# Attention and gated feed-forward on one core: six blocks' queries behind the context, and the looks, one weight sum and the second block's attention placed anew

## The chip, the cores and the metric

One core of a Trainium2 chip. The metric is the device time of one launch in microseconds; a lower one is better. TensorE (PE) multiplies matrices into PSUM, VectorE (DVE), ScalarE (ACT) and GpSimd (POOL) work elementwise, SyncE (SP) issues the transfers.

## The reference

Linear attention (no softmax) over 4096 tokens of width 256, a residual sum and a layer norm, then a gated feed-forward net and a second residual sum and norm. "tlin" is a product with a weight matrix, then a scale for each output channel.

```python
# x: (1, 4096, 256); wq, wk, wv: (64, 256); wo: (256, 64)
Q = x @ wq.T;  K = x @ wk.T;  V = x @ wv.T
energy = einsum('bnd,bne->bde', K, V)
context = einsum('bnd,bde->bne', Q, energy) * sqrt(3 / 64)
x = layernorm(x + context @ wo.T)
h = silu(tlin(x, w1, s1)) * tlin(x, w2, s2)            # hidden width 1024
h = gelu(tlin(h, h1, sh1)); h = gelu(tlin(h, h2, sh2)) # exact gelu
x = layernorm(x + tlin(h, w3, s3))
```

All weights of the feed-forward net are small integers, and wq is plus or minus 1/16.

## The kernel before, in words

The tokens are eight blocks of 512. Every engine runs a list of instructions written out by hand, and semaphores alone tie the lists together: an engine stands at an instruction until its semaphores have come, and all behind it stands too. SP's list of transfers is one such list.

**Two-part products.** An operand is split into a rounded high part (ScalarE: hi, high_x, hi_of_q, hi_of_transposed) and a low rest (VectorE: lo, low_x, lo_of_q, lo_of_transposed). TensorE multiplies both with weights that are exact in the short format. Whether they are, the kernel looks itself: ScalarE sums the low bits of each piece of weights (`bits`, L562: bits_of_w12, bits_of_whole for loaded units, bits_of_sums for sums of weights). For each of seven stages TensorE adds the sums up (flag_sum, L1203), VectorE makes a flag of them (flag_out, L864), and TensorE loads it (load_flag, L1215) and jumps by it (stages_from, L1225).

**Front** (L1417). For each block f: keys and values (kv_products, L1150), copied by VectorE, and their energy, one 64 x 64 sum over all blocks (energy, L1166). Queries are four matmuls a block, two on xhi and two on xlo (q_pieces, L1134; piece n belongs to block n // 4). Up to `Q_BETWEEN` a block's queries stand between two rounds of keys and values. Behind the last energy come T1 (energy times wo, L1430) and the attention of block 0, tile by tile (attention_tile, L1178; a tile is 128 tokens, and there are four in a block). VectorE adds x and takes the statistics of each tile (normalised_tilewise, L1057), GpSimd makes the inverse deviation and the shift (L483, L477), ScalarE normalises tiles 0 and 1 (normalise_tile, L627), VectorE tiles 2 and 3, and TensorE transposes each tile (transposed_first, L1449). Block 1's attention is done in two halves (attention_half, L1453) among them. The queries of the other blocks are copied out by ScalarE (raw_q, L602), those of blocks 4 to 7 on their way to DRAM.

**Gate layer** (l1, L1251): sixteen tiles of four matmuls for a block, half of them for silu (ScalarE, L633), half for the gate (VectorE, L932). Tile t >= 4 needs a bank that silu or gate has left (l1_free, L1238). Within block 0's layer, behind tile 9, stand the transposes of block 1 (L1197, TR1_AFTER); they need it normalised (stats and normalise on VectorE, L905 and L924, with inverse_deviation on GpSimd between them, L454).

**Hidden layers.** Two 1024 x 1024 products for two blocks at a time, each by seven products of half size with sums of weights and of activations (product, L1298; differences, L499). The sums of weights are made once: GpSimd combines a loaded unit in four operations (combine, L439), SP stores it to DRAM (store_unit, L319), and each product loads its sum into one of three ring slots (load_ring, L324). Two of seven products take a quarter of the weights unchanged, which SP copies from DRAM to DRAM (relay_hidden, L307).

In the `combine` and in ScalarE's list the order that matters below is this:

```python
combine(0)                                   # GpSimd
inverse_deviation_tilewise(0)
combine(1)
inverse_deviation(0, 1)
pool.wait_ge(norm_done[0], 1)
combine(2)
```

## Time and profile before

| | |
|---|---|
| median of 3 runs | 653.43 us (651.85 to 653.5) |
| the profiled execution, its own time | 653.65 us |
| its span | 651.9 us |
| TensorE busy | 637.2 us, 98% of the span |
| VectorE, ScalarE, GpSimd busy | 485.7, 410.7 and 282.1 us |
| granted TensorE clock | 0.998 of full speed |
| moved by DMA | 103.89 MB, 159 GB/s over the span |

In a timeline a line is a run of like instructions: start, length, engine, line of the code, what is written from what, how many, and in brackets how long the engine had been idle and who released it. "idle" is shown from about 0.15 us on. Lengths of neighbouring instructions on ScalarE and VectorE overlap by about 0.1 us, so distances between starts are the better measure.

### The profile page before, as it was taken

Reading aid. Unit: us, or ns where it says so; the run is one execution under the profiler, and the core shown is the slowest. Engines: PE = TensorE matmul, PEld = TensorE weight load, DVE = VectorE, ACT = ScalarE, POOL = GpSimd, SP = SyncE. Lnnn points to the kernel's source line nnn. Section 1 sums busy time; section 2 is a strip of 40 time slices with the busy share of each in tenths; the row PEclk is TensorE's granted clock in tenths of the full one; section 3 lists DMA queues with packets and bytes.
Section 4 is the critical chain, followed back from the end, with each engine's and each line's share of the span. In section 5 each row is a group of like instructions: output and inputs, shape, how many; then the busy total and the mean of one; then the engine's idle time right before and its main releaser. Section 6 shows DMA issues by size and latency. Waiting matters only on the chain.

```text
span 651.9 us, 9251 instructions
## 1 busy us (share of the span) xinstructions
PE 637.2 (98%) x3191; PEld 534.6 (82%) x3191; DVE 485.7 (75%) x717; ACT 410.7 (63%) x696; POOL 282.1 (43%) x226
## 2 busy tenths in 40 slices
PE   8989999999999999999999999999999999999995
PEld 6867788878889888888889888888889888888885
DVE  4677598789664997798655898698754899488476
ACT  5488789658761666557662657656763457666554
POOL 0367999295000663097000565079000367068034
PEclk9999999999999999999999999999999999999999
DMA  8989999764320036633330035734330015444201
GB/s 327 394 325 341 372 380 348 285 255 164 130 67 1 1 118 220 211 130 130 130 129 1 1 97 167 250 126 168 130 129 2 1 28 188 173 135 160 94 1 66
DMA packets 24370, 103.89 MB, mean 159 GB/s; under 512 B 2224, under 2 KB 3312, under 8 KB 16496
## 3 DMA queue, kind: packets, MB, share of 16 engines
q1 hardware_dynamic: 24032, 102.98, 44.5%
q8 instruction: 29, 0.48, 0.3%
q10 hardware_dynamic: 288, 0.26, 0.1%
q14 instruction: 21, 0.17, 0.1%
HBM read 87.51 MB, written 23.07 MB: 170 GB/s over the span
## 4 chain that ended last, share of the span: by engine, by line
PE 72%; DVE 3%; POOL 1%; issue 1%; ACT 1%; POOLq 0%; DVEq 0%; ACTq 0%
PE ps L1322 49%; PE ps L1262 13%; PE ps L1376 8%; DVE R L944 1%; DVE xr L928 1%; PE ps L1194 1%; PE ps L1182 1%; PE ps L1399 0%; ACT R L674 0%; DVE U L963 0%; POOL rstd L488 0%; POOL quarter L516 0%; ACT quarter L720 0%; POOL rstd L459 0%; POOL quarter L525 0%
## 5 line engine op out<-in xcount | busy, mean ns | idle before, releaser
L1322 PE MATMUL ps<-R,ring 128*128 128x512 f32 x1792 | 410.1, 390 | 1.6 <-DVE fsum L866 1.2
L1322 PEld LDWEIGHTS ps<-R,ring 128*128 128x128 f32 x1792 | 335.2, 188 | 71.6 <-DVE fsum L866 1.6
L944 DVE TENSOR_TENSOR R<-quarter,R 128x512 fp32r<-128x512 f32 x284 | 261.8, 944 | 62.6 <-ACT R L674 62.2
L674 ACT CAST R<-quarter 128x512 fp32r<-128x512 f32 x288 | 175.4, 616 | 30.6 <-POOL quarter L516 12.6
L1262 PE MATMUL ps<-x1T,w 128*128 128x512 f32 x512 | 119.4, 391 | 1.9 <-ACT sg L640 1.1
L720 ACT ACTIVATE quarter<-U,sc 128x512 f32<-128x512 f32 x96 | 69.5, 724 | 74.2 <-DVE U L963 29.4
L1262 PEld LDWEIGHTS ps<-x1T,w 128*128 128x128 f32 x512 | 95.2, 188 | 23.8 <-ACT sg L640 2.7
L506 POOL TENSOR_TENSOR quarter<-quarter,quarter 128x512 f32<-128x512 f32 x32 | 49.6, 1550 | 97.8 <-ACT quarter L720 91.1
L457 POOL TENSOR_TENSOR ve<-mv,eps 128x4 f32<-128x4 f32 x14 | 5.7, 404 | 181.5 <-DVE mv L921 181.5
L640 ACT ACTIVATE sg<-ps,sc 128x512 f32<-128x512 f32 x64 | 44.0, 689 | 61.3 <-PE ps L1262 61.1
L690 ACT COPY U<-ps 128x512 f32<-128x512 f32 x96 | 56.3, 586 | 31.3 <-PE ps L1322 31.3
L938 DVE SCALAR_TENSOR_TENSOR quarter<-ps,sc,sg 128x512 f32<-128x512 f32 x64 | 47.8, 746 | 23.7 <-ACT sg L640 13.4
L516 POOL TENSOR_TENSOR quarter<-quarter,quarter 128x512 f32<-128x512 f32 x32 | 48.9, 1527 | 16.7 <-DVE quarter L938 12.9
L1376 PEld LDWEIGHTS ps<-w,R 128*128 128x128 f32 x448 | 54.7, 192 | 0.7 <-DVE R L944 0.2
L1376 PE MATMUL ps<-w,R 128*128 128x256 f32 x448 | 55.1, 283 | 0.0
L528 POOL TENSOR_TENSOR quarter<-quarter,quarter 128x512 f32<-128x512 f32 x32 | 50.0, 1594 | 0.0
L525 POOL TENSOR_TENSOR quarter<-quarter,quarter 128x512 f32<-128x512 f32 x32 | 48.8, 1554 | 0.0
L928 DVE TENSOR_SCALAR xr<-xr,mv,rstd 128x256 f32<-128x256 f32 x52 | 35.5, 743 | 4.2 <-POOL rstd L459 4.2
L957 DVE TENSOR_TENSOR U<-ps,U 128x512 f32<-128x512 f32 x32 | 22.0, 690 | 14.7 <-PE ps L1322 14.7
L720 ACT ACTIVATE quarter<-ps,sc 128x512 f32<-128x512 f32 x32 | 22.1, 691 | 12.6 <-PE ps L1322 12.6
L963 DVE TENSOR_TENSOR U<-ps,U 128x512 f32<-128x512 f32 x32 | 21.8, 685 | 8.2 <-PE ps L1322 8.2
L446 POOL TENSOR_TENSOR beside<-unit 128x512 f32<-128x512 f32 x8 | 12.2, 1530 | 29.8 <-ACT junk L569 27.7
(84 smaller groups left out, 383.4 us busy)
## 6 DMA issues: line engine op xcount, KB each, us to landing
ring<-combos SPq DMA_DIRECT2D x56, 1024.0 KB, 4.9
combos<-unit SPq DMA_DIRECT2D x8, 1024.0 KB, 7.1
unit<-in_h1T SPq DMA_DIRECT2D x4, 1024.0 KB, 13.9
xr<-in_x_rows SPq DMA_DIRECT2D x8, 512.0 KB, 6.2
unit<-in_h2T SPq DMA_DIRECT2D x4, 1024.0 KB, 12.7
xT<-in_xT SPq DMA_DIRECT2D x7, 512.0 KB, 8.6
out<-xr SPq DMA_DIRECT2D x7, 512.0 KB, 2.9
w<-w_dram SPq DMA_DIRECT2D x3, 1024.0 KB, 7.5
```

What stands on the lines that cost most here:

```text
L506: nc.gpsimd.tensor_tensor(x12[:, c, :], x12[:, c, :], x11[:, c, :], ALU.subtract).then_inc(t_done, 1)
L516: nc.gpsimd.tensor_tensor(t2[:, c, :], x22[:, c, :], x12[:, c, :], ALU.subtract).then_inc(t_done, 1)
L525: nc.gpsimd.tensor_tensor(x11[:, c, :], t2[:, c, :], x11[:, c, :], ALU.subtract).then_inc(t_done, 1)
L528: nc.gpsimd.tensor_tensor(x21[:, c, :], x21[:, c, :], t2[:, c, :], ALU.subtract).then_inc(t_done, 1)
L674: nc.scalar.copy(R[slot_of(p, u)][:, 0, c, :], quarter[operand_home(p, u)][:, c, :]).then_inc(hi_done, 1)
L690: nc.scalar.copy(U[:, 1 if i == 2 else 0, j, :], ps[:, B + j, :]).then_inc(cp_done, 1)
L720: nc.scalar.activation(quarter[dst][:, j, :], src, ACT.Gelu, scale=sc[:, 2 + l, chunk:chunk + 1]).then_inc(gelu_done, 1)
L938: nc.vector.scalar_tensor_tensor(quarter[dst][:, j % KH, :], ps[:, base + (2 * j + 1) % 4, :], sc[:, 1, j:j + 1], sg[:, j % 2, :], ALU.mul ...
L944: nc.vector.tensor_tensor(r[:, 1, c, :], quarter[operand_home(p, u)][:, c, :], r[:, 0, c, :].bitcast(f32), ALU.subtract).then_inc(lo_done, 1)
L1262: last = nc.tensor.matmul(ps[:, base + t % 4, :], w, view(x1T[beta % 2][:, part, c, :]), start=n == 0, stop=n == 2 * EC - 1)
L1322: last = nc.tensor.matmul(ps[:, bank + j, :], w, view(R[slot_of(p, u)][:, part, k, :]), start=n in (0, 1, 5) and k == 0 and part == 0, sto ...
L1376: last = nc.tensor.matmul(rows_of(b)[:, q, :], view(slot[:, part, k, q * P:(q + 1) * P]), w, start=first and k == 0 and part == 0 and q % ...
```

## The change

**TensorE.** Only block 0's queries and block 1's stand between the rounds of keys and values; those of blocks 2 to 7 follow the last energy. Fifteen of the 24 come before the first transposed tile, three between it and tile 1's, four behind. The jump by the look at w12 stands behind them, ahead of tiles 2 and 3 and of block 1's attention, whose halves change places. Block 6's queries go to bank 2. In product 5 of each first hidden layer the attention of the next two blocks stands behind its third and fourth part in place of behind all four.

**ScalarE.** The casts of x no longer wait for queries (eight buffers in place of four, the last four in the ring's space). raw_q(2) and raw_q(3) stand around a look at w12, behind T1; the normalised tiles 0 and 1 stand behind all looks at w12; the look at unit 1 behind raw_q(7); the looks at sums are split in two; hi_of_q(2) and hi_of_q(3) go to the first hidden layer.

**GpSimd.** The last of unit 0's four operations waits until block 0 is normalised.

**VectorE.** The flag of w12 comes ahead of the normalising of tiles 2 and 3; lo_of_q(2) and (3) go to the first hidden layer.

**SP.** Block 0's rows of x go ahead of unit 0. The two DRAM copies of a hidden layer are apart, each with a flag of its own, and the second comes behind the first ring load, or behind block 2's rows. The ring's first load waits for all queries. Units 5 and 6 go behind ring load 2, unit 7 behind ring load 3.

```diff
-Q_BETWEEN = 4
+Q_BETWEEN = 2
-Q_BANK = (4, 5, 6, 7, 5, 4, 5, 3)
+Q_BANK = (4, 5, 6, 7, 5, 4, 2, 3)
...
+        xhi_at = [x1T_at + 4096 * i for i in range(4)] + [ring_at + 4096 * i for i in range(4)]
+        xhi = [over(f"xhi{f}", xhi_at[f], [P, EC, BLK], f32r) for f in range(NB)]
...
+                if g == 0:
+                    sp.wait_ge(q_ready, NB)
+                if L < 2 and n < 2:
+                    sp.wait_ge(hidden_relayed[L][n], 16)
...
+            load_rows(0)
             load_unit(0)
             load_w12(0)
             load_w12(1)
-            load_rows(0)
...
-            relay_hidden(0)
+            relay_hidden(0, 0)
             load_unit(4)
             store_unit(2)
             load_ring(0)
+            relay_hidden(0, 1)
+            store_unit(3)
             load_ring(1)
+            load_ring(2)
             load_unit(5)
-            store_unit(3)
             load_unit(6)
-            load_ring(2)
+            load_ring(3)
             load_unit(7)
             store_unit(4)
-            load_ring(3)
-            relay_hidden(1)
             load_ring(4)
+            relay_hidden(1, 0)
             load_rows_late(2)
+            relay_hidden(1, 1)
...
             combine(0)
             inverse_deviation_tilewise(0)
+            pool.wait_ge(last_norm[0], TPB - ACT_TILES[0])
+            last_sum(0)
             combine(1)
...
                 silu(0, j, A)
-                if j == 1:
-                    hi_of_q(2)
-                if j == 3:
-                    hi_of_q(3)
                 if j == 0:
                     bits_of_whole(2)
-                if j == 2:
-                    bits_of_sums(0)
+                if 2 <= j <= 3:
+                    bits_of_sums(0, range(j - 2, j - 1))
...
-                if j == 6:
+                if j == 5:
                     bits_of_whole(3)
...
                 silu(1, j, A)
-                if j == 0:
-                    bits_of_sums(1)
+                if j <= 1:
+                    bits_of_sums(1, range(j, j + 1))
...
-                if j == 1:
+                if j == 2:
                     bits_of_whole(4)
-                if j == 4:
-                    bits_of_sums(2)
+                if 3 <= j <= 4:
+                    bits_of_sums(2, range(j - 3, j - 2))
...
-                q_pieces(range(23, 28), view)
+                q_pieces(range(15, 25), view)
                 pe.wait_ge(q_raw, 2)
                 transposed_first(0)
-                q_pieces(range(28, 30), view)
-                transposed_first(1)
-                q_pieces(range(30, 32), view)
+                q_pieces(range(25, 28), view)
                 pe.wait_ge(tile_sum[0], 1)
                 flag_sum(1)
-                transposed_first(2)
-                attention_half(0)
-                transposed_first(3).then_inc(tr_ready, 1)
-                attention_half(1).then_inc(op_ready, 1)
+                transposed_first(1)
+                q_pieces(range(28, 32), view)
...
+                transposed_first(2)
+                attention_half(1)
+                transposed_first(3).then_inc(tr_ready, 1)
+                attention_half(0).then_inc(op_ready, 1)
                 l1(0, A, view, side)
```

TensorE from the sum of the look at w12 on, before (L1194 are transposed tiles, L1182 block 1's attention, L1217 and L1230 the flag's load and the jump):

```order
L1211 MATMUL ps<-lowf,ones 1x4 [waits bits_done,tile_sum0]
L1194 MATMUL ps<-ident,xr 128x128 [waits last_norm0]
L1194 MATMUL ps<-ident,xr 128x128
L1182 MATMUL ps<-T1s,qs_66 128x256 [waits q_raw,qlo_done]
L1182 MATMUL ps<-T1s,qs_66 128x256 x3
L1194 MATMUL ps<-ident,xr 128x128 [waits last_norm0]
L1194 MATMUL ps<-ident,xr 128x128
L1182 MATMUL ps<-T1s,qs_66 128x256 [waits q_raw,qlo_done]
L1182 MATMUL ps<-T1s,qs_66 128x256 x3
L1217 TENSOR_LOAD flag [waits flag_done]
L1217 ISA x2
L1230 COMPARE_AND_BRANCH
```

And in the change (the same lines are L1216, L1199, L1187, L1222 and L1235 there, the queries L1150):

```order
L1216 MATMUL ps<-lowf,ones 1x4 [waits bits_done,tile_sum0]
L1199 MATMUL ps<-ident,xr 128x128 [waits tile_norm0]
L1199 MATMUL ps<-ident,xr 128x128
L1150 MATMUL ps<-xhi_116,wqr 128x512 [waits tile_sum0,xhi_done]
L1150 MATMUL ps<-xhi_116,wqr 128x512
L1150 MATMUL ps<-xlo_124,wqr 128x512 [waits xlo_done]
L1150 MATMUL ps<-xlo_124,wqr 128x512
L1222 TENSOR_LOAD flag [waits flag_done]
L1222 ISA x2
L1235 COMPARE_AND_BRANCH
L1199 MATMUL ps<-ident,xr 128x128 [waits last_norm0]
L1199 MATMUL ps<-ident,xr 128x128
```

The jump has moved from behind the transposed tiles and the attention to ahead of tile 2; tile 1 and four query matmuls now stand ahead of it.

ScalarE from T1 to the first silu, before (L569 are looks, L605 copies of queries, L631 normalised tiles, L625 the cast of the transposed block):

```order
L801 ACTIVATE T1s<-ps 128x256 [waits t1_ready]
L605 COPY q_stage_95<-ps 128x512 [waits q_ready]
L569 ACTIVATE junk,lowf<-w_49 128x1024 [waits bits_done,w12_in1] x2
L605 COPY q_stage_96<-ps 128x512 [waits q_ready]
L631 ACTIVATE xr<-xr,shift,rstd_84 128x256 [waits shift_done] x2
L569 ACTIVATE junk,lowf<-unit_122 128x1024 [waits bits_done,unit_in1]
L605 COPY q_stage_97<-ps 128x512 [waits q_ready]
L625 CAST x1T_63<-ps 128x512 [waits tr_ready]
L625 CAST x1T_63<-ps 128x512
L605 COPY q_stage_98<-ps 128x512 [waits q_ready]
```

And in the change, from the copy behind T1 on (looks L580, copies L614, normalised tiles L640, cast L634):

```order
L614 COPY xr<-ps 128x512 [waits q_ready]
L580 ACTIVATE junk,lowf<-w_49 128x1024 [waits bits_done,w12_in0]
L614 COPY xr<-ps 128x512 [waits q_ready]
L580 ACTIVATE junk,lowf<-w_49 128x1024 [waits bits_done,w12_in1] x2
L640 ACTIVATE xr<-xr,shift,rstd_84 128x256 [waits shift_done]
L614 COPY q_stage_95<-ps 128x512 [waits q_ready]
L640 ACTIVATE xr<-xr,shift,rstd_84 128x256 [waits shift_done]
L614 COPY q_stage_96<-ps 128x512 [waits q_ready]
L634 CAST x1T_63<-ps 128x512 [waits tr_ready]
L634 CAST x1T_63<-ps 128x512
L614 COPY q_stage_97<-ps 128x512 [waits q_ready]
L614 COPY q_stage_98<-ps 128x512 [waits q_ready]
```

The first normalised tile now stands behind two copies and three looks, counted from T1, and the look at unit 1, which stood ahead of the cast, comes behind these rows.

## Rows read from the trace of the kernel before

**Rows 1.** Busy time of a stretch: us, engines' busy us, granted clock, DMA.

```profile
150.00:600.00 450.00, 449.70 (x2200) 380.03 (x2200) 342.61 (x501) 272.60 (x464) 167.09 (x120) 1.00 0.33 113
```

**Rows 2.** TensorE's waits by line: us in total, times, longest.

```profile
PE ps L1322 <- DVE fsum L866: 1.2, 1, 1.2
...
PE ps L1322 <- issue: 0.4, 1, 0.4
```

**Rows 3.** TensorE's timeline: start, us, instruction, xcount, [idle before].

```profile
18.54 1.95 PE L1162 MATMUL ps<-wkv,xT 128*128 128x128 f32 x16
...
22.05 1.95 PE L1162 MATMUL ps<-wkv,xT 128*128 128x128 f32 x16
...
24.54 2.05 PE L1162 MATMUL ps<-wkv,xT 128*128 128x128 f32 x16
...
27.12 2.05 PE L1162 MATMUL ps<-wkv,xT 128*128 128x128 f32 x16
...
34.07 0.40 PE L1145 MATMUL ps<-xlo,wqr 128*128 128x512 f32 x1
...
36.77 0.41 PE L1194 MATMUL ps<-ident,xr 128*128 128x128 f32 x2 [1.37 <-ACT xr L631]
...
39.55 0.38 PE L1194 MATMUL ps<-ident,xr 128*128 128x128 f32 x2
...
41.08 9.53 PE L1262 MATMUL ps<-x1T,w 128*128 128x512 f32 x40 [0.68 <-ACT x1T L625]
50.45 1.03 PE L1194 MATMUL ps<-ident,xr 128*128 128x128 f32 x8
51.24 13.23 PE L1262 MATMUL ps<-x1T,w 128*128 128x512 f32 x56
65.55 4.85 PE L1262 MATMUL ps<-x1T,w 128*128 128x512 f32 x20 [1.08 <-ACT sg L640]
```

**Rows 4.** ScalarE's timeline.

```profile
33.10 1.06 ACT L569 ACTIVATE junk<-w 128x1024 uint8<-128x1024 uint16 x1
...
35.40 0.57 ACT L605 COPY q_stage<-ps 128x512 f32<-128x512 f32 x1
...
39.96 1.07 ACT L625 CAST x1T<-ps 128x512 fp32r<-128x512 f32 x2 [0.67 <-PE ps L1194]
...
58.47 1.90 ACT L569 ACTIVATE junk<-unit 128x2048 uint8<-128x2048 uint16 x1
...
61.12 0.60 ACT L674 CAST R<-quarter 128x512 fp32r<-128x512 f32 x1
...
62.21 0.61 ACT L674 CAST R<-quarter 128x512 fp32r<-128x512 f32 x1
63.77 1.06 ACT L569 ACTIVATE junk<-unit 128x1024 uint8<-128x1024 uint16 x1 [0.95 <-DMA unit<-in_h2T]
```

**Rows 5.** The flag's load near 39.5 us: ns min/median/max, first and last start.

```profile
L1217 PEldq TENSOR_LOAD <-flag x1: 906/906/906, 39.5 to 39.5; - x1
```

**Rows 6.** GpSimd's timeline: tile 0's shift, combine(1), an inverse deviation, an operation of combine(4).

```profile
35.73 0.27 POOL L480 TENSOR_SCALAR shift<-mv,rstd 128x1 f32<-128x1 f32 x1
...
38.96 1.41 POOL L446 TENSOR_TENSOR beside<-unit 128x512 f32<-128x512 f32 x1 [0.19 <-ACT junk L569]
...
43.17 1.29 POOL L452 TENSOR_TENSOR unit<-unit 128x512 f32<-128x512 f32 x1
...
46.34 1.02 POOL L459 TENSOR_TENSOR rstd<-ve,nhalf 128x4 f32<-128x4 f32 x1
...
69.85 1.61 POOL L452 TENSOR_TENSOR unit<-unit 128x512 f32<-128x512 f32 x1
```

**Rows 7.** VectorE's timeline: normalise of block 1.

```profile
48.03 1.37 DVE L928 TENSOR_SCALAR xr<-xr,mv,rstd 128x256 f32<-128x256 f32 x4
```

**Rows 8.** SP's timeline: issue of unit 4's load.

```profile
50.58 0.75 SPq L317 DMA_DIRECT2D unit<-in_h2T  x1
```

**Rows 9.** Transfers issued near 50.6 us: KB each, us to landing.

```profile
unit<-in_h2T SPq DMA_DIRECT2D x1, 1024.0 KB, 13.2
```

More of the change, by code:

```diff
@@ L148, in build @@
         xT = [over(f"xT{f}", r_at + 4096 * f, [P, TPB * E]) for f in range(NB)]
-        xhi = [over(f"xhi{i}", x1T_at + 4096 * i, [P, EC, BLK], f32r) for i in range(4)]
+        xhi_at = [x1T_at + 4096 * i for i in range(4)] + [ring_at + 4096 * i for i in range(4)]
+        xhi = [over(f"xhi{f}", xhi_at[f], [P, EC, BLK], f32r) for f in range(NB)]
         xlo = [over(f"xlo{f}", r_at + 4096 * f, [P, TPB * E], f32r) for f in range(NB)]
@@ L180, in build @@
         unit_out = [sem(f"unit_out{i}") for i in range(NU)]
-        hidden_relayed = [sem(f"hidden_relayed{l}") for l in range(2)]
+        hidden_relayed = [[sem(f"hidden_relayed{l}_{h}") for h in range(2)] for l in range(2)]
         ring_in = [sem(f"ring_in{k}") for k in range(SLOTS)]
@@ L439, in combine @@
             def combine(i):
-                w11, w21, w12_, w22 = (unit[i][:, a, :] for a in range(4))
+                w11, w21, _, w22 = (unit[i][:, a, :] for a in range(4))
                 pool.wait_ge(unit_in[i], 16)
@@ L450, in combine, with last_sum @@
                 nc.gpsimd.tensor_tensor(w11, w21, w11, ALU.subtract).then_inc(combo_step, 1)
+                if i != 0:
+                    last_sum(i)
+            def last_sum(i):
                 pool.wait_ge(combo_step, 3 * i + 3)
-                nc.gpsimd.tensor_tensor(w12_, w12_, w11, ALU.subtract).then_inc(combos_made, 1)
+                nc.gpsimd.tensor_tensor(unit[i][:, 2, :], unit[i][:, 2, :], unit[i][:, 0, :], ALU.subtract).then_inc(combos_made, 1)
             def inverse_deviation(ln, n):
@@ L786, in _ @@
             nc.scalar.copy(wqr[:, :, :], wq[:, :, :]).then_inc(wq_rounded, 1)
-            for f in range(4):
+            for f in range(5):
                 high_x(f)
             hi_of_q(0)
-            high_x(4)
+            high_x(5)
             hi_of_q(1)
-            high_x(5)
-            raw_q(2)
             high_x(6)
-            raw_q(3)
             high_x(7)
@@ L798, in _ @@
             bits_of_w12(0)
-            bits_of_w12(1)
             act.wait_ge(t1_ready, 1)
             nc.scalar.activation(T1s[:, 0, :], ps[:, 3, 0:E], ACT.Copy, scale=CTX_SCALE).then_inc(t1_hi, 1)
-            raw_q(4)
+            raw_q(2)
+            bits_of_w12(1)
+            raw_q(3)
             bits_of_w12(2)
             bits_of_w12(3)
+            normalise_tile(0, 0, 0, 1, tile_norm[0])
+            raw_q(4)
+            normalise_tile(0, 0, 1, 2, tile_norm[0])
             raw_q(5)
-            for q in range(ACT_TILES[0]):
-                normalise_tile(0, 0, q, q + 1, tile_norm[0])
+            hi_of_transposed(0, 6)
+            raw_q(6)
+            raw_q(7)
             bits_of_whole(1)
-            raw_q(6)
-            hi_of_transposed(0, 6)
-            raw_q(7)
             act.wait_ge(cst_in, 16 * NCST)
@@ L980, in hidden @@
                         add_first(L, j)
+                    if L == 0 and j < 2:
+                        lo_of_q(a + j)
                     if j > 0:
@@ L1005, in hidden @@
                         add_fourth(L, j)
-                    if L == 0 and j == 1:
+                    if L == 0 and j == 2:
                         residual1(a, B)
@@ L1325, in product @@
                     last.then_inc(prod, 1)
+                    if side is not None:
+                        side(j)
             def hidden(p, l, view):
@@ L1345, in with_sums, with attention @@
                 product(p, l, 4, view)
-                product(p, l, 5, view)
-                if l == 0 and more:
-                    for i in range(2):
-                        pe.wait_ge(gelu_done, n_gelu(L, 1, 2 * i + 1))
-                        attention_out(a + i, lambda q, at=B + 2 * i: ps[:, at + q // 2, q % 2 * E:(q % 2 + 1) * E])
+                def attention(j):
+                    if j >= 2:
+                        pe.wait_ge(gelu_done, n_gelu(L, 1, 2 * j - 3))
+                        attention_out(a + j - 2, lambda q, at=B + 2 * (j - 2): ps[:, at + q // 2, q % 2 * E:(q % 2 + 1) * E])
+                product(p, l, 5, view, attention if l == 0 and more else None)
                 if p == 0 and l == 1:
```

43 lines of the change are left out of this document (19 added, 24 removed).

## The prediction

> **What bounds the kernel now.** I read the busy time by stretch first. From 150 to 600 us TensorE is busy for 449.70 of 450 us, at a granted clock of 1.00 [rows 1]: in the body nothing but its own matmuls counts, and the change removes none of them. What can be won or lost is idle time of TensorE outside that stretch. The list of its waits names one at the flag sum of the second layer, 1.2 us, and 0.4 us of issue at a stage's start [rows 2]; its timeline shows the others, all early [rows 3]: 1.37 us before the first transposed tile (36.77), 0.68 before the first gate layer (41.08), 1.08 in that layer's second block (65.55). These five are 4.7 us, 0.7% of the span: the most that could be won, were every one to go. A change under 0.3%, some 2 us, can't be told from none here.
>
> **1. The context comes earlier.** A round of keys, values and energy takes 3.51 us with one block's queries in it (18.54 to 22.05), 2.49 just behind such a round (22.05 to 24.54) and 2.58 in a pure run (24.54 to 27.12) [rows 3]. Blocks 2 and 3 leave two rounds, so 3.51 + 3.51 + 2.49 become 2.49 + 2.58 + 2.58: **1.87 us earlier** for everything that hangs on the context: T1, attention of block 0, its sums and statistics. Waits for x don't eat this: by then the last x transfer is long there, and the eight xhi tiles no longer wait for queries. The rows of x go ahead of unit 0 on SP's queue, so unit 0 and both halves of w12 land 512 KB (about 1.3 us) later. They still come before ScalarE must turn to T1, though with only some 0.3 us to spare.
>
> **2. Most of that lead is lost on ScalarE.** It must normalise tile 0 before TensorE can transpose it. Before, both looks at w12's second half (33.10 to 35.40, 2.30 us) lay in time in which the tile's shift wasn't there yet [rows 4]. Now the shift, ready at 36.00 before [rows 6], is there at 34.1, but the order puts ahead of it raw_q(2), a look, raw_q(3) and these two looks. raw_q(3) needs the last query matmul of block 3, which stands where the one of 34.07 stood [rows 3]: 34.07 - 1.87 = 32.2, and the copy can start at about 32.6 and is through at 33.1. Then 2.30 of looks: 35.4; the tile 0.6: 36.0; TensorE starts tile 0 at **36.15** in place of 36.77. From 32.2 TensorE has ten query matmuls of 0.24 (13.23 / 56 [rows 3]), to 34.6, and then idles 1.5 us: the old wait stays.
>
> **3. From there to tile 3.** Before, it was 39.55 - 36.77 = 2.78. Now three query matmuls more lie in it (0.7), 0.2 of waiting for tile 1 goes, and the jump into the next stage stands ahead of tile 2, so that it lies in the chain: load of the flag, compare, branch. No row shows that jump with nothing beside it. Ends: 0.4 us (the issue wait [rows 2]) and 0.9 (the flag's TENSOR_LOAD took 906 ns [rows 5]); I take 0.7, by the 0.68 before 41.08, in which the same look's jump lies. A wait for the flag is not added: flag_sum(1) stands seven instructions ahead, and VectorE now waits for it before it normalises tiles 2 and 3, which are wanted only behind the jump. So tile 3 starts at 36.15 + 2.78 + 0.7 - 0.2 + 0.7 = 40.15, **0.6 later** than before, and the gate layer, which hangs on tile 3 through the casts and the low halves on VectorE, moves by the same 0.6. The trace decides this price against a rule: in the Trainium skill, Advanced Engine Details and Errata, Control Flow Timing, a compare-and-branch is about 108 ns. The compare alone agrees, but what counts here is the load with it. By that rule the jump would be 0.1, and the sum 0.6 lower.
>
> **4. The second block's transposes.** They stand behind ten tiles of the gate layer, reached at 50.45 before, with no wait [rows 3]; now at 51.05. They need block 1 normalised, and its inverse deviation is behind combine(1) on GpSimd, which needs the look at unit 1; combine(1) began at 38.96 [rows 6]. Now ScalarE does it last: tile 3's transpose 40.15; casts 0.41 later (39.55 to 39.96) and 1.07 long; raw_q(6) and raw_q(7), 0.57 each; the look 1.15 (half of 2.30) [rows 4]: 43.9, GpSimd 44.0. combine(1) took 5.50 (38.96 to 44.46); at 1.61 an operation it would be 6.5 [rows 6], and I take 5.5, since what VectorE does beside it is again gates and statistics with PSUM inputs. The inverse deviation is 1.3 (0.28 + 1.02), normalise 1.37 [rows 6, 7]: 44.0 + 5.5 + 1.3 + 1.4 + 0.1 = 52.3. TensorE **waits 1.25 us** where it did not wait. The point for gate(3), queued behind normalise on VectorE, is 54: not reached. The Trainium skill, SBUF — State Buffer, Who interferes with whom, has a VectorE instruction with two SBUF inputs block a GpSimd read altogether; none stands in this stretch, so by it combine(1) would be 4 x 1.37 = 5.5 as well, and the 6.5 is what a lo beside it would cost.
>
> **5. The wait at 65.55 goes: -1.08.** silu(1, 2) was late because ScalarE stood 0.95 us for unit 4 (63.77) [rows 4]. unit 4 now has one relay of 1 MB ahead of it instead of two, and the look stands one silu later; two query casts have left ScalarE and VectorE there.
>
> **6. A new wait in the same place.** ScalarE starts the second block's first silu a tile (0.945: 13.23 over 14 [rows 3]) and 0.2 after TensorE starts the block. Tile 12 needs silu(1, 4), and ahead of its end now lie four silu-and-hi pairs of 1.09, both parts of sums(1) 2.65, the look at unit 4 1.05, the long part of sums(2) 2.0 and the silu 0.67 [rows 4]: 10.7. That is 12.0 with the handover, against 12 x 0.945 = 11.3: **+0.65**.
>
> **7. At nothing.** The queries' casts in the second layer's start (ScalarE and VectorE, 1.2 and 1.4 us) lie beside product matmuls with some 3 us in hand, and so does unit 5, which lands some 10 us later. The attention of two blocks moves into product 5 with the same matmuls; VectorE's residuals wait less. If this cover were gone, product 3 would wait by what is missing. The wait at the flag sum, 1.2 us, hangs on TensorE's own product 6, VectorE's add, gelu and eight GpSimd differences, all behind that product, so it moves with it and stays.
>
> Sum: +0.6 + 1.25 - 1.08 + 0.65 = **+1.4 us**. Profiled execution 653.65 + 1.4 = 655.05; it stands 0.22 above the median, 653.43: **654.8**.
>
> **Rivals.** (a) The lead is kept. Were tile 0 ready when TensorE is (34.7 in place of 36.15), tile 3 and the gate layer would come 0.85 earlier than before, and with combine(1) in time and tile 12 free, -0.85 - 1.08 = -1.9 is left: 651.5; with a jump of 0.1 it is 650.9. For it: T1 1.87 earlier is sure. Against it: ScalarE's order is fixed, and the 2.30 of looks can't be passed. Chance 0.12, most of which would have to come through some step that I priced too high. (b) Slower by more than 2 us, through the transfers. store_unit(0) leaves behind last_sum(0), which waits for block 0's last norm and takes another 1.3 us: some 40. store_unit(1) leaves behind combine(1), at 49.5 in place of 44.5 [rows 6]. unit 4 landed 50.58 + 13.2 = 63.8, 19.3 behind store_unit(1) [rows 8, 9]. With a relay less I expect 15.4 behind it, 64.9, wanted at 65.8. Were the relay to save nothing, it would land at 68.8 and hold ScalarE, and so tile 12, for 3 us: 657.8. It decides from 0.9 us of delay on; ring(1), behind the second relay and with 1.5 us in hand, adds to it. Chance 0.28, with combine(1) at 6.5 or a second long wait counted in. (c) The Control Flow rule holds, as a mechanism: the flag is loaded while the queries still run, and the jump is hidden. Then tile 3 comes at 39.55, the four terms are 0, 1.25, -1.08 and 0.65, and the time is 654.2. Chance 0.15, inside no change. (d) That the change doesn't do what it says: only if the rounds were held by x; but from 18.54 to 27.12 they follow each other with no idle time shown [rows 3], so under 0.02.
>
> **Numbers.** Forecast, within 0.3%: 0.60, with 653 to 656 as its own range. Faster 0.12, slower 0.28. Range: down to 651.5, where half of (a) is left out; up to 657.5, which takes most of (b).
>
> **What the profile after would show.** Key and value rounds of 2.5 us and T1 at 29.4; ScalarE's first normalised tile at 35.4 directly behind a look; TensorE idle about 1.4 us before the first transposed tile and 0.4 to 0.9 before the third, with the flag's load there; the gate layer's first matmul at 41.5 to 41.7; a wait of 1 to 1.5 us at the second transposes, named after VectorE's normalise; none by unit 4; one of about 0.7 before tile 12 of the second block, released by silu. A first transposed tile at 35 would make step 2 wrong, no wait at the second transposes step 4, a ScalarE look released by a DMA near 66 would be rival (b).

## The result, and the profile after

The changed kernel takes 655.4 us (median of 7 runs, 655.02 to 656.32), the one before 653.43 in the runs beside it (651.85 to 654.22). The ratio is 1.0039, with a 95% interval of 1.0028 to 1.0050, or 1.8 to 3.3 us slower; it is estimated from all the runs and isn't the ratio of the two medians, which is 1.0030. The forecast was 654.8, inside no change. So the total is 0.6 off, and by the forecast's own line of 0.3% the kernel is slower, though the interval begins just under that line. Profiled spans are 653.6 and 651.9; I account for these 1.7 us, since the rows come from them.

The stretch in which nothing was to happen, 150 to 600 us (columns as in [rows 1], 449.70 busy before):

```profile
150.00:600.00 450.00, 448.83 (x2195) 379.06 (x2194) 340.87 (x500) 270.99 (x463) 165.77 (x119) 1.00 0.33 113
```

TensorE's timeline after, the rows that answer to [rows 3], and then the waits behind 140 us:

```profile
14.54 1.95 PE L1167 MATMUL ps<-wkv,xT 128*128 128x128 f32 x16
...
17.03 2.05 PE L1167 MATMUL ps<-wkv,xT 128*128 128x128 f32 x16
...
19.62 2.05 PE L1167 MATMUL ps<-wkv,xT 128*128 128x128 f32 x16
...
28.90 0.70 PE L1439 MATMUL ps<-wo,ET 64*128 64x256 f32 x2
...
32.10 0.40 PE L1150 MATMUL ps<-xlo,wqr 128*128 128x512 f32 x1
...
36.04 0.41 PE L1199 MATMUL ps<-ident,xr 128*128 128x128 f32 x2 [1.37 <-ACT xr L640]
...
39.22 0.38 PE L1199 MATMUL ps<-ident,xr 128*128 128x128 f32 x2
...
40.37 9.91 PE L1267 MATMUL ps<-x1T,w 128*128 128x512 f32 x40 [0.30 <-ACT x1T L634]
51.12 1.06 PE L1199 MATMUL ps<-ident,xr 128*128 128x128 f32 x8 [0.84 <-DVE xr L934]
...
51.94 16.60 PE L1267 MATMUL ps<-x1T,w 128*128 128x512 f32 x72
69.16 1.20 PE L1267 MATMUL ps<-x1T,w 128*128 128x512 f32 x4 [0.62 <-ACT sg L649]
...
73.28 5.60 PE L1327 MATMUL ps<-R,ring 128*128 128x512 f32 x24
```
```profile
142.08 16.66 PE L1327 MATMUL ps<-R,ring 128*128 128x512 f32 x72 [1.54 <-DVE fsum L872]
...
183.17 7.04 PE L1267 MATMUL ps<-x1T,w 128*128 128x512 f32 x30 [0.18 <-issue]
...
310.90 1.06 PE L1199 MATMUL ps<-ident,xr 128*128 128x128 f32 x8 [0.44 <-DVE xr L934]
```

Rounds follow each other in 2.49 and 2.59 us, the gate layer starts at 40.37 with 0.30 of idle time, the second transposes wait 0.84, tile 12 of the second block 0.62, and nothing waits for unit 4. Three waits are new or longer behind 140 us: 1.54 at the flag sum (1.16 in before's timeline), 0.44 at 310.90, and another 0.43 a pair later, at 461.51. One of 0.18 stands ahead of the second pair's gate layer, put down to issue: time in which the engine waited for nothing that the profile shows.

To set the two runs side by side I count from the third round of keys and values, which began at 11.51 before and 11.02 after, since x came at different times (in the kernels with the change's front it began anywhere from 11.00 to 12.09). The balance, each stretch as after minus before (product 0 is the first product of the first hidden layer, the "first pair" runs from there to the gate layer of the second pair):

| stretch | before | after | difference | forecast |
|---|---|---|---|---|
| start to 3rd round | 11.51 | 11.02 | -0.49 | |
| to the first transposed tile | 25.26 | 25.02 | -0.24 | -0.62 |
| to the gate layer | 4.31 | 4.33 | +0.02 | +1.2 |
| to the second transposes | 9.37 | 10.75 | +1.38 | +1.25 |
| to product 0 | 23.41 | 22.16 | -1.25 | -0.43 |
| first pair | 108.98 | 109.89 | +0.91 | 0 |
| from there to w3's row near 642 | 458.23 | 459.55 | +1.32 | 0 |

They sum to +1.65. The front (rows two to five) was forecast at +1.4 and comes out at -0.09; the loss lies behind it, in what I had put at nothing. These are single executions. In e1, e3, e10, e11 and e14 below, which have the front of the kernel after, product 0 starts 61.90 to 62.26 behind the third round, and 62.26 to 62.35 in the kernel before, e2 and e9, which have the old one. So the front wins between nothing and 0.45 us.

### The profile page after: what moved, and what is told of

It reads as the page before. It is cut to its first block and busy times, and to the rows that moved or that the text cites. A ratio compares the mean times of both kernels' runs of the same rounds, so it can differ in the third digit from the quotient of the medians.

```text
span 653.6 us, 9254 instructions
## 1 busy us (share of the span) xinstructions
PE 638.0 (98%) x3191; PEld 534.5 (82%) x3191; DVE 485.4 (74%) x717; ACT 408.8 (63%) x696; POOL 280.5 (43%) x226
## 5 line engine op out<-in xcount | busy, mean ns | idle before, releaser
L580 ACT ACTIVATE junk<-unit 128x1024 uint8<-128x1024 uint16 (+1 forms) x16 | 23.9, 1494 | 9.4 <-DMA unit<-in_h1T 9.4
```

## The experiments

"The weave" is the change's new order in product 5, with the attention of the next two blocks between and behind its last two parts. All ratios are against the kernel before, which took 652.48 to 653.43 in its sets of runs. Theory A is that VectorE's and ScalarE's work, put elsewhere in the hidden layers, is late and holds TensorE there; its rivals are given with each.

### The weave alone and the change without it

VectorE's timeline near product 5 of the second pair, after:

```profile
272.44 0.69 DVE L963 TENSOR_TENSOR U<-ps,U 128x512 f32<-128x512 f32 x1 [1.50 <-PE ps L1327]
...
275.04 2.35 DVE L897 TENSOR_TENSOR xr<-ps,xr 128x1024 f32<-128x1024 f32 x2
...
309.38 1.37 DVE L934 TENSOR_SCALAR xr<-xr,mv,rstd 128x256 f32<-128x256 f32 x4
```

and before:

```profile
271.16 0.69 DVE L957 TENSOR_TENSOR U<-ps,U 128x512 f32<-128x512 f32 x1 [0.53 <-PE ps L1322]
...
273.76 2.35 DVE L891 TENSOR_TENSOR xr<-ps,xr 128x1024 f32<-128x1024 f32 x2
...
308.10 1.37 DVE L928 TENSOR_SCALAR xr<-xr,mv,rstd 128x256 f32<-128x256 f32 x4
```

The pair's product 0 started at 227.64 after and at 227.34 before, so each of these three links (part 3's sum, block a's and b's residual sums, block b's normalise) is 0.98 us later against it. Half of the attention now runs on TensorE ahead of part 3 of product 5 (the fourth and last, counted from 0), and everything behind part 3's sum follows. e1 puts the attention back in the kernel after; e2 makes this one edit in the kernel before, together with the one on VectorE that belongs to it in the change: block a's residual sum one step later in the first pair.

```diff
 e1, against after:
-                product(p, l, 5, view, attention if l == 0 and more else None)
+                product(p, l, 5, view)
+                if l == 0 and more:
+                    attention(2)
+                    attention(3)
```

> The changed kernel with the attention of two blocks back behind all of product 5. Theory A (the weave makes VectorE's chain late): in pairs 1 and 2 the attention of the first block delays the product's last part by 0.95 us, and with it VectorE's last low half, both residual sums, all that follows, and the second transposes of the next layer; the waits of 0.44 and 0.43 us there go, each pair is 0.65 us shorter, 1.3 us in all: about 654.1. Rival B (the loss behind 300 us is TensorE's own, from switching between two kinds of matmul twice as often): the switching goes too, so this run alone gives the same 654.1, but without the waits it removes TensorE's busy time would have to fall. Rival C (transfers or the front are the cause): no change from 655.4.

> The kernel before with nothing but the weave of the attention into product 5 (and VectorE's first residual sum one step later in the first pair). Theory A: +1.3 us in pairs 1 and 2, nothing or up to 0.5 in the first pair: 654.7 to 655.2, with a wait of about 0.4 at the second transposes of each later pair. Rival C: no change from 653.4.

e1: 654.53, ratio 1.0021 (1.0012 to 1.0029). e2: 654.19, 1.0017 (1.0006 to 1.0027). TensorE's timeline at the second pair's second transposes, without the weave (e1):

```profile
310.20 1.91 PE L1199 MATMUL ps<-ident,xr 128*128 128x128 f32 x16
```

and with the weave alone (e2):

```profile
310.33 1.06 PE L1194 MATMUL ps<-ident,xr 128*128 128x128 f32 x8 [0.46 <-DVE xr L928]
```

Counted from product 0 to the first matmul behind the second transposes, the two later pairs take 84.1 us each with the weave and 83.4 without, from either side (e1 83.42 and 83.43; e2 84.10 and 84.07; before 83.42 twice, after 84.08 and 84.07). So the weave costs 0.65 a pair, 1.3 in all, and it is shown by undoing it and by doing it alone. In the first pair the weave changes nothing in the kernel before: its last product starts 101.35 behind product 0 in e2 and 101.30 before.

In time e1 won less than the 1.3: its first pair took 110.65 for the 109.89 of the kernel after. Of this, 0.69 is a wait for the rows of x of block 3, which were issued at 113.43 and at 113.01 in the kernel after. Whether the missing weave has a part in that isn't shown; e4 below has the weave and waits 0.61 there. Both medians were off their forecasts by about half a microsecond (654.1, and 654.7 to 655.2), so it is the pairs in the traces that show the 0.65, with the medians in line.

### The weave with VectorE's sums ahead

If the late link is VectorE's order and not TensorE's, taking block a's and b's residual sums ahead of the last low half should win the time back with the weave in place.

```diff
                 for j in range(KH + 1):
                     if j < KH:
                         add_fourth(L, j)
...
+                    if l == 0 and p > 0 and more and j == KH:
+                        residual1(a, B)
+                        residual1(b, B + 2)
                     if j > 0:
                         lo(p, u0 + 7, j - 1)
-                if l == 0 and p > 0 and more:
-                    residual1(a, B)
-                    residual1(b, B + 2)
```

> The changed kernel, weave kept, but in pairs 1 and 2 VectorE adds the two residuals ahead of the last low half instead of behind it, in time in which it waits for ScalarE anyway. Theory A: VectorE is about 1.3 us earlier from there, the waits at the second transposes go, 1.3 us less: 654.1. Rival B (TensorE's own switching): the weave is still there, so no change from 655.4.

654.54, 1.0021 (1.0012 to 1.0029). The pairs are 83.45 and 83.44, with no wait: so the late link is the order on VectorE. But the first pair took 111.04, with a new wait. Its timeline, and the transfers issued between 100.5 and 100.9 us (KB each, us to landing):

```profile
111.87 5.72 PE L1327 MATMUL ps<-R,ring 128*128 128x512 f32 x24 [1.74 <-issue]
```

```profile
ring<-combos SPq DMA_DIRECT2D x1, 1024.0 KB, 11.1
```

Ring load 5 was issued at 100.64, landed at 111.7, and product 5 wanted it at 110.1. In the kernel after it went at 100.56 and took 9.0: there by half a microsecond. Before, it went at 97.76 and took 8.6: there more than four early. The change has used up this transfer's reserve, and then an execution in which it takes 1 to 2 us more pays for it (below, e5 paid 0.61). e3 doesn't touch this stretch.

### The queries between the rounds again

```diff
-Q_BETWEEN = 2
+Q_BETWEEN = 4
...
-                q_pieces(range(8, 10), view)
+                q_pieces(range(16, 18), view)
...
-                q_pieces(range(10, 15), view)
+                q_pieces(range(18, 23), view)
...
-                q_pieces(range(15, 25), view)
+                q_pieces(range(23, 25), view)
```

> The changed kernel with the queries of blocks 2 and 3 back between the rounds of keys and values, all else as changed. If the context's place is what made the front 0.58 us shorter in spite of two new waits, everything from T1 to the gate layer's end comes later by what ScalarE's fixed list makes of it: T1 1.9 later, the first transposed tile 1.5 later (37.6), the gate layer's end 1.5 later: 656.9. Rival: the looks on ScalarE hide the context's lead, and the front stays as it is to within 0.3: 655.4.

658.37, 1.0075 (1.0059 to 1.0092), 1.5 above the forecast. The first transposed tile came at 37.73 and product 0 at 76.49 instead of 73.28. Of these 3.21 us, 0.92 is x, which came late in this execution (third round at 11.94). Another 0.77 is the first transposed tile, counted from the third round (25.79 for 25.02). The rest, 1.45, lies between this tile and the gate layer (5.78 for 4.33), and there TensorE ran at a lower clock:

```profile
36.62 0.47 PE L1150 MATMUL ps<-xhi,wqr 128*128 128x512 f32 x1 [1.70 <-DVE xr L1083]
37.73 0.41 PE L1199 MATMUL ps<-ident,xr 128*128 128x128 f32 x2 [0.64 <-ACT xr L640]
...
39.08 1.11 PE L1150 MATMUL ps<-xhi,wqr 128*128 128x512 f32 x2
```

Two query matmuls took 1.11 us here and 0.71 in the kernel after (37.40). The granted clock was 0.60, 0.50, 0.50 and 0.70 in the four microseconds from 39 on, behind idle times of 1.70 and 0.64 us that lay close together; 0.50 is the lower level, 1.2 GHz. The kernel after has 1.37 of idle time there and the full clock. Four microseconds at a mean of 0.57 are up to 1.7 us of lost clock, so the 1.45 is accounted for. The place of the two blocks' queries was worth 0.7 to 1.1 us to the first transposed tile (it stands 24.66 to 25.06 behind the third round in the ten traces with the queries where the change has them). The forecast had 1.5 for that and nothing for the clock. Of the other five executions the one with the lowest mean clock, 0.992, took 659.90, and the two with the highest, 0.997, took 658.14 and 656.46. Pair and flag waits were those of the kernel after (0.44, 0.47, 1.55).

### The jump in its old place

```diff
                 q_pieces(range(28, 32), view)
+                transposed_first(2)
+                attention_half(1)
+                transposed_first(3).then_inc(tr_ready, 1)
+                attention_half(0).then_inc(op_ready, 1)
...
-                transposed_first(2)
-                attention_half(1)
-                transposed_first(3).then_inc(tr_ready, 1)
-                attention_half(0).then_inc(op_ready, 1)
                 l1(0, A, view, side)
```

> The kernel after, with the second block's tiles 2 and 3 and its two attention halves back ahead of the jump, so that nothing but the gate layer stands behind the jump, as before. Theory (a jump costs where the flag is read late): before, the flag's load took 906 ns and 0.68 us stood open at the gate layer; here the flag comes early, as in the kernel after (load of 0.31 us), so the wait at the gate layer stays under 0.3 us, its first matmul starts at 40.2 to 40.5 and the time is that of the kernel after, 1.002 to 1.004 of before. Rival (a jump costs what it costs wherever weight loads follow it, and the rounds behind it merely paid it in the kernel after): 0.6 to 0.8 us open at the gate layer, its first matmul at 40.9 to 41.2, and the ratio 0.001 above the kernel after's.

The gate layer started at 39.93 with 0.29 of idle time; counted from the third round that is 28.93, and 29.35 in the kernel after. The flag's load, after, in e5, and before in [rows 5] (906 ns):

```profile
L1222 PEldq TENSOR_LOAD <-flag x1: 311/311/311, 37.7 to 37.7; - x1
```

```profile
L1222 PEldq TENSOR_LOAD <-flag x1: 312/312/312, 38.1 to 38.1; - x1
```

From ScalarE's first cast of the transposed block to the gate layer's first matmul it is 0.73 us in both, and 1.12 before (39.96 to 41.08). So the jump costs nothing there in either place, it did cost some 0.4 before, and the theory is right that its place isn't what made it dear. What makes a load last 0.3 or 0.9 us is not settled: it follows the flag by 0.2 us before (flag at 39.3) as in the kernel after (37.5), and by 0.9 in e5 (37.2). All kernels with the change have the short load, e4 with its queries moved back too: 308 to 323 ns here and 302 to 418 at the next stage. The kernels before, e2 and e9 have the long one, 898 to 913 and 862 to 1169. The time was 655.67, 1.0055 (1.0041 to 1.0069), not under the kernel after's: here too the time went behind the stretch tried, 0.61 at ring load 5 (110.48) and 0.81 at tile 12.

### The look at unit 1 earlier

ScalarE stood idle 2.30 us ahead of its cast near 39.6 in the kernel after, and had the look at unit 1 behind it. e6 is e1 with this:

```diff
             raw_q(5)
+            bits_of_whole(1)
             hi_of_transposed(0, 6)
             raw_q(6)
             raw_q(7)
-            bits_of_whole(1)
```

> The kernel without the weave (654.5) and with ScalarE's look at h2's unit 1 ahead of its cast of tile 6's high part, into the 2.30 us that ScalarE stood idle there. Theory: the look starts some 2 us earlier (39.6 instead of 41.55), combine(1) on GpSimd starts at 41.0 instead of 42.9 and is over before the second block is normalised, so the wait of 0.84 us at 51.1 goes: 653.7, ratio 1.0008. Rival: VectorE's normalisation is slowed by something else than the combine (its reads of the rows), so the wait stays within 0.3 of 0.84 and the time at 654.5. Second rival: the look holds the cast of tile 6, and the gate layer's first groups wait for it instead, by 0.5 or more.

653.36, 1.0015 (1.0006 to 1.0024): 0.0006 below e1. The second transposes:

```profile
50.05 1.03 PE L1199 MATMUL ps<-ident,xr 128*128 128x128 f32 x8
```

No wait, and product 0 starts 61.08 behind the third round instead of 61.91. The wait of step 4 was combine(1), as forecast, and one move takes it away. The two intervals of the ratio overlap, so it is the trace that shows this.

### The first pair: three tries and an ablation

The kernel before with one edit, to see whether the wait for fsum can be had:

```diff
-                    if L == 1 and j == KH - 1:
+                    if L == 1 and j == 1:
                         flag_out(5)
```

> The kernel before with one edit: VectorE sends flag_out(5) behind its second residual of the second layer and not behind its last. Theory: the wait of 1.16 us for fsum at 141.8, which the kernels before and after both have, goes whole, since fsum(5) had long been added up; nothing behind it is late: 651.7, ratio 0.998. Rival: what follows the jump needs VectorE's residuals themselves, which are in order behind the flag, and the wait only moves there: 652.8, ratio 1.000.

653.83, 1.0014 (1.0005 to 1.0023). The rival was right that the wait only moved, and it came back dearer.

```profile
150.60 7.55 PE L1322 MATMUL ps<-R,ring 128*128 128x512 f32 x32 [1.25 <-ACT U L690]
...
159.66 1.06 PE L1194 MATMUL ps<-ident,xr 128*128 128x128 f32 x8 [0.64 <-DVE xr L928]
```

A wait at a flag may be a chain that is late anyway: 1.16 went at 141.8, and 1.25 and 0.47 (0.64 for 0.17 before) came behind it.

e10 is e1 with SyncE's second copy for a hidden layer ahead of block 2's rows:

```diff
-            load_rows_late(2)
             relay_hidden(1, 1)
+            load_rows_late(2)
```

> The kernel without the weave (654.5), and on SyncE's queue the relay of h2's unit 6 half ahead of the late load of block 2's rows instead of behind it. Theory (block 3's rows come late since the queue ahead of them stands behind block 2's rows, issued only at 99.6): the relay goes at 89.6 as soon as the one ahead of it, ring load 5 and store of unit 5 earlier, block 3's rows are issued 1 to 2 us earlier than 113.4, and the 0.69 us wait for the second sum at 125.4 goes or falls under 0.2: 653.9, ratio 1.0011. Rival: the store of unit 5 is bound by the look at it, not by the queue, so that block 3's rows are issued at 113 still and the wait stays: 654.5, ratio 1.0021.

655.24, 1.0039 (1.0026 to 1.0053). The wait for block 3's rows went, as expected of the queue, but the flag's wait grew to 1.86, and behind it TensorE was slow (e10; columns as in [rows 1]):

```profile
140.00:145.00 5.00, 3.14 (x10) 2.47 (x10) 3.24 (x7) 1.71 (x3) 4.84 (x7) 0.77 0.21 80
145.00:150.00 5.00, 5.00 (x21) 4.07 (x20) 4.51 (x6) 4.00 (x8) 5.00 (x4) 0.89 0.60 210
150.00:155.00 5.00, 5.00 (x23) 4.13 (x22) 5.00 (x4) 3.69 (x7) 5.00 (x4) 1.00 0.22 49
```

```profile
141.93 18.23 PE L1327 MATMUL ps<-R,ring 128*128 128x512 f32 x72 [1.86 <-DVE fsum L872]
```

The 72 matmuls took 18.23 us, in the other kernels that wait there 16.62 to 16.66. The granted clock was 0.50, the lower level of 1.2 GHz, from 143 to 146.

e11 moves the queries' casts and residuals of blocks 2 and 3, which the change had brought into the first pair, into gaps of ScalarE and VectorE; e12 does the same in e6, and e13 is e12 with e10's edit.

```diff
 ScalarE, and VectorE in the same way with lo_of_q ahead of its fourth lo:
                 for j in range(KH):
                     copy_out(L, 0, j)
+                    if L == 0 and j == KH - 1:
+                        hi_of_q(2)
+                        hi_of_q(3)
                     hi(p, u0 + 2, j)
-                if L == 0:
-                    hi_of_q(2)
-                    hi_of_q(3)
```

> The kernel after, weave and all, with the queries of blocks 2 and 3 in the first pair put elsewhere: ScalarE's two casts (1.14 us) between its fourth copy out of product 0 and the cast behind that, where it stood idle 1.81 us for GpSimd, and VectorE's two residuals (1.07 and 0.95) ahead of its fourth residual of product 2, where it stood idle 1.84. Theory (the 0.9 us that the first pair grew by came from these four instructions: behind them ScalarE's gelus, the looks at h2's units and with them SyncE's queue all ran 1.5 to 2 us later against product 0): first pair, from product 0's start to the second pair's gate layer, 108.9 to 109.2 instead of 109.89; the flag's wait in the second layer back from 1.54 to 1.2; time 0.0012 of before's less than the kernel after's: ratio 1.0025. Rival (the first pair grew because GpSimd's combine of unit 4 ended later against product 0, 71.70 with product 0 at 73.28 instead of 71.43 with 73.86): ScalarE and VectorE still follow GpSimd's quarters, the pair stays at 109.7 to 110, ratio as the kernel after's.

> The same move in the kernel without the weave and with the early look at unit 1 (653.36, 1.0015; its first pair 110.50). Theory as before: the wait for the second sum (0.36) and 0.4 of the flag's wait go, the first pair falls by 0.9 or more to 109.6 or less: 652.3, ratio 0.9995 to 1.0002. Rival: 110.2 to 110.5, ratio 1.0015.

> The same with the relay of h2's unit ahead of the late load of block 2's rows as well. Alone, this relay took the wait for block 3's rows away but left a flag's wait of 1.86, behind which TensorE's granted clock fell (0.77 and 0.89 in the two stretches of 5 us from 140) and 72 matmuls took 18.23 us and not 16.64. Theory: with ScalarE early the flag's wait is 1.3 or less, the clock stays at 1.00, and the first pair is 108.8 to 109.2: 651.8 to 652.2, ratio 0.999. Rival (the clock falls with the relay's place, not with the wait): 18 us again and 110.5, ratio 1.0015.

e11: 656.41, 1.0051 (1.0038 to 1.0065), first pair 110.65: a miss. VectorE's timeline in e11 and in the kernel after:

```profile
82.62 3.38 DVE L881 TENSOR_TENSOR qs<-xr,qs 64x512 fp32r<-64x512 f32 x2
```

```profile
85.89 1.07 DVE L880 TENSOR_TENSOR qs<-xr,qs 64x512 fp32r<-64x512 f32 x1
...
87.71 0.95 DVE L880 TENSOR_TENSOR qs<-xr,qs 64x512 fp32r<-64x512 f32 x1
```

In the gap the two residuals took 3.38 us and not 2.0, so VectorE was no earlier behind them. Besides, ScalarE stood 1.14 us for a unit's load at 85.54, ahead of its first gelu. e12: 652.96, 1.0007 (0.9998 to 1.0016), first pair 110.02 where e6 has 110.50. That is no gain of the move either: the last product starts 102.46 behind product 0 in e12 and 102.42 in e6, and the 0.48 is idle time put down to issue ahead of the gate layer, 0.53 in e6 and none in e12. This time is 0 to 0.60 from trace to trace, 0.18 in the kernel after and none in the one before, and nothing here explains it. e13: 653.67, 1.0008 (0.9999 to 1.0017), first pair 109.96. Both forecasts, 109.6 or less and 108.8 to 109.2, were missed. In e13 the flag's wait was 1.86 again and the clock stayed up:

```profile
141.67 16.62 PE L1329 MATMUL ps<-R,ring 128*128 128x512 f32 x72 [1.86 <-DVE fsum L873]
```

So neither the relay's place nor a wait of this length brings the clock down for certain. e10's slow stretch is shown, its cause isn't. Six more executions of e13 had a mean clock of 0.995 or 0.996, where e10's traced one had 0.996, so the clock may have fallen in them too; no trace of them is kept.

What e10 and e13 do show is the chain behind the 0.91. In the kernel after, VectorE's residual sum of block 3 waits for that block's rows of x:

```profile
123.52 1.23 DVE L897 TENSOR_TENSOR xr<-ps,xr 128x1024 f32<-128x1024 f32 x1 [0.83 <-DMA xr<-in_x_rows]
```

and before:

```profile
122.54 1.22 DVE L891 TENSOR_TENSOR xr<-ps,xr 128x1024 f32<-128x1024 f32 x1
```

It did not wait there. SyncE issued these rows in the kernel after 39.73 us behind product 0 (37.56 before), and they took 10.4 (10.0). The flag behind this sum is 52.76 behind product 0 for 51.87, which is 0.89 later, and from it to the flag at 142 it is 16.02 in the kernel after and 16.01 before: the whole delay goes through to TensorE. With the rows in time, in e10 and e13, the first of these flags is at 51.87 and 51.85, as before, but the second follows in 16.6: VectorE then waits 1.29 us for ScalarE where it waited 0.70. So two chains are late, one over the transfers by 0.9 and one over ScalarE by 0.6, and removing the first alone wins 0.3.

e14 cuts these casts and residuals from 512 to 8 columns in the kernel after and leaves the rest of the two blocks' queries out, with all orders and waits kept.

```diff
+                n = 8 if b in (2, 3) else BLK
-                nc.scalar.copy(qs[b % 2][:, :], ...
+                nc.scalar.copy(qs[b % 2][:, 0:n], ...
```

> The kernel after, with ScalarE's casts and VectorE's residuals of the queries of blocks 2 and 3 cut from 512 to 8 columns (the rest of these queries is left out, so those two blocks' attention is computed from what stood there). Order, waits and every other instruction stay. Theory (the 2 us of residuals that the change put among VectorE's work in product 1 of the first pair, where VectorE then has no idle time until 108, are what makes the first pair longer; moving them into a gap beside GpSimd's additions did not help since there they took 3.38 us): the four instructions shrink to 0.1 to 0.2 us each, ScalarE's first gelu starts at 86.3 instead of 87.5, the second layer's flag wait falls from 1.54 to 1.2, the first pair from 109.89 to 109.0 to 109.3, and the ratio is 0.001 under the kernel after's. Rival (GpSimd's combine of unit 4 and the quarters behind it, which end 1.15 later against product 0 than before): the gelus follow GpSimd, the first pair stays at 109.7 or more.

654.59, 1.0029 (1.0017 to 1.0041), 0.001 under the kernel after, which the intervals do not separate. The first pair took 109.35, just over the theory's range, and the first gelu started 13.40 behind product 0 (14.24 after, 12.04 before). But the flag's wait stayed at 1.52, where the theory had 1.2. Of the 0.54 that the pair is shorter, 0.15 is less issue time ahead of the gate layer and not of this work; up to the last product it is 101.77, for 102.16 after and 101.30 before. So this work is some 0.4 of the 0.9, by one trace of each. It goes through the transfers: block 3's rows were issued 38.83 behind product 0 (39.73 after), and the flag behind their sum is at 52.38 (52.76). e14 doesn't take all of the work away: the two residuals of 8 columns still took 0.54 and 0.50 of what had been 1.07 and 0.95. Whether the other 0.5 is that remainder, the new order on SyncE or GpSimd is open: GpSimd's second group of differences begins 10.14 behind product 0 after (83.42) and 8.99 before (82.85), since combine(4) began later against product 0, and no run here moves that, or SyncE's order, alone.

## Why the forecast was nearly right in time and wrong in its reasons

The total, 0.6 us off, is luck: two errors of 1.5 and 2.2 us with opposite signs. The steps in turn:

**Step 1 held.** Rounds of 2.49 and 2.59, T1 at 28.90: 1.84 us earlier against the third round (31.23 before), for 1.87. The margin of 0.3 at the looks did not hold: ScalarE stood 1.34 us at 29.15 for w12's first half, and T1's copy came some 0.6 later than its matmul allowed.

**Step 2 held in kind.** The first transposed tile at 36.04 for 36.15, behind an idle time of 1.37: the looks ahead of tile 0 eat the lead. The number is helped by x, which came 0.49 earlier: against the third round the tile is 0.24 earlier than before, for 0.62 forecast.

**Step 3 failed, and rival (c) was right there.** "I take 0.7" for the jump was wrong: the 906 ns of [rows 5] and the 0.68 of [rows 3] belong to the kernel before and not to a jump as such. Ahead of tile 2 it measured nothing (38.48, right behind the queries), and at the next stage the load fell from 1169 to 308 ns and the 0.39 of issue, [rows 2], went too. The gate layer was forecast 1.2 later against the first transposed tile and came 0.02 later: 1.2 of the 1.5 us that the front did better. TensorE's sequencer still worked some 0.6 us on it, from the load at 37.7 to the end of the branch, but with query matmuls queued ahead TensorE did not stand. The rule in the Trainium skill, Advanced Engine Details and Errata, Control Flow Timing, gave the better forecast; I had overruled it with a row that showed a wait. The compare-and-branch itself took 69 ns before and 71 after, for the 108 ns of the page, so "the compare alone agrees" holds only in size.

**Step 4 held in kind.** 10.75 from the gate layer to the transposes for 10.62 forecast (9.37 + 1.25), but differently made up: a wait of 0.84, named after VectorE's normalise, and 0.5 in the layer's first ten tiles, in rows too small to be listed as waits. e6 shows the cause of the first. Of the second 0.4 is left in e6 (9.77 for 9.37), and its cause is open.

**Steps 5 and 6 held.** No wait for unit 4; tile 12 waits 0.62 for silu, 0.65 forecast. The stretch to product 0 was still 0.82 better than forecast: 0.39 is the issue time of the next jump (step 3), and some 0.4 is again in rows too small to be listed. Rival (b) did not happen at unit 4, though it was right that transfers had lost their reserve: block 3's rows and ring load 5 did.

**Step 7 failed, twice.** "The attention of two blocks moves into product 5 with the same matmuls; VectorE's residuals wait less" counted matmuls and residuals. It left out VectorE's sum of part 3, which stands behind the attention on TensorE and ahead of a chain that ends at block b's normalise. Cost: 0.65 a pair, 1.3 in all. And "the queries' casts lie beside product matmuls with some 3 us in hand" took TensorE's reserve at one place. VectorE had none: from 84.14 to 109 us it idles 0.20 and 0.25 us and no more, so 2 us of residuals went through to its sums, ScalarE's gelus and looks at units, and with them SyncE's stores and loads, down to block 3's rows. Cost: some 0.4 of 0.91, by e14. The other 0.5 is shown as a delay (rows issued 2.17 late against product 0, ScalarE 0.6 late), but not which of the change's moves made it. Front 1.5 too dear, hidden layers 2.2 too cheap: the good total is the luck named above.

## What to carry to other kernels

"Beside other work" is a statement about one engine. Before a step is moved at no cost, follow what stands behind it on its own engine to the next place where TensorE waits, at every repetition of the loop, not only in the first. A wait is worth removing only if the chain that comes next is not late as well (e9), and what an operation took in one order of the work is not its price in another (e5). No kernel tried here beats the one before: the best, e12, is at 1.0007 (0.9998 to 1.0016), with the weave undone, and the look at unit 1 and the queries' casts and residuals placed anew.

## What the runs showed of the hardware

- The seven loads of a flag took 0.30 to 0.49 us in the kernel after, with a median of 0.31, and up to 1.17 in the one before. Beside the matmuls queued at 37.7 the short one cost TensorE no idle time that shows. At later stages, with loads just as short (300 to 308 ns), idle times of 0.17 and 0.18 put down to issue stand in the kernel after, and 0.53 and 0.60 in e6 and e11.
- The same elementwise subtraction with both inputs in SBUF on VectorE took 0.68 us (128 x 512) at 273.05, with GpSimd idle, and 1.11 at 84.14 and 1.58 at 88.78, while GpSimd worked. One of 64 x 512 took 1.07 and 0.95 there (85.89 and 87.71), and cut to 64 x 8 it still took 0.54 and 0.50 (e14). The Trainium skill, SBUF — State Buffer, Who interferes with whom, says that such an instruction and a GpSimd read keep each other out; the trace agrees.
- Behind a wait of 1.86 us the granted clock was 0.77 and 0.89 in two stretches of 5 us in one kernel (e10, 72 matmuls in 18.23 us), and 1.00 in another with the same wait (e13, 16.62).
- In e4, behind idle times of 1.70 and 0.64 us within 3 us, the granted clock was 0.50 to 0.70 from 39 to 43 us. That stretch cost 1.45 us; the kernel after, with one wait of 1.37 there, kept the full clock.
- The same 1 MB load, issued near 100 us, took from 6.3 (e13) to 11.1 us (e3) to land.
